# Shared cross attention: the row maxima turned by four products on column tiles instead of one transpose

## The reference

```python
q = (x @ Wq + bq)   # 16 heads of 16
k = (context @ Wk + bk)
v = (context @ Wv + bv)
scores = einsum('bhqd,bhkd->bhqk', q, k) / 4
attn = softmax(scores, axis=-1)
x = x + merge(einsum('bhqk,bhkd->bhqd', attn, v)) @ Wo + bo
```

## Time and profile before

| | |
|---|---|
| median of three executions | 1522.3 us |
| profiled execution | 1522.39 us |
| its span | 1520.6 us |
| TensorE busy | 1368.7 us, 90% |
| weight loads busy | 1059.2 us, 70% |
| DVE busy | 765.3 us, 50% |
| ACT busy | 643.5 us, 42% |
| 32 transposes of the maxima, each of three layers | 0.276 us median each |

### The profile page before, as it was taken

How to read it: one execution, slowest core, us unless ns; L and a number is a source line. 1 busy time by engine, 2 the same in 40 slices (tenths; PEclk the granted TensorE clock), 3 DMA queues, 4 the chain that set the end, 5 groups by cost and what they waited for, 6 DMA issues and landing times. The chain is left out here.

```text
span 1520.6 us, 31526 instructions
## 1 busy us (share of the span) xinstructions
PE 1368.7 (90%) x12506; PEld 1059.2 (70%) x12506; DVE 765.3 (50%) x1723; ACT 643.5 (42%) x1680; POOL 198.1 (13%) x197
## 2 busy tenths in 40 slices
PE   7999899989989899999999869989967896799887
PEld 6776667866556677879999755669964575577632
DVE  3666677655556676500000475600127485477565
ACT  3444226633366266234444235532224674166300
POOL 3000260000034300041111200040032000400000
PEclk9999999999999999899999978999998997799999
DMA  6000340011301200467994100364211000600100
GB/s 213 1 1 1 68 68 16 3 43 42 78 8 21 51 4 3 154 225 274 348 346 169 35 22 1 132 254 163 103 47 49 1 2 1 110 11 3 67 1 22
DMA packets 43943, 120.19 MB, mean 79 GB/s; under 512 B 11931, under 2 KB 28440, under 8 KB 38412
## 3 DMA queue, kind: packets, MB, share of 16 engines
q1 hardware_dynamic: 33048, 62.04, 14.2%
q0 software_dynamic: 7616, 53.12, 10.1%
q10 hardware_dynamic: 3136, 3.03, 0.6%
HBM read 95.78 MB, written 11.00 MB: 70 GB/s over the span
## 5 line engine op out<-in xcount | busy, mean ns | idle before, releaser
L798 PE MATMUL wide<-early_kt,early_q 32*100 32x361 f32 x512 | 96.6, 490 | 2.7 <-PEq L66 1.5
L2533 ACT ACTIVATE l1f_hidden<-wide,l1f_pack 128x128 f32<-128x128 f32 x160 | 58.8, 368 | 78.0 <-PE wide L2472 68.1
L2635 DVE TENSOR_TENSOR l1f_out<-summed,l1f_pack 128x256 f32<-128x256 f32 x20 | 8.5, 425 | 156.8 <-PE summed L2480 156.8
L113 PE MATMUL summed<-ident 128*128 128x128 f32 x320 | 46.8, 315 | 35.9 <-PEq L66 35.9
L2472 PEld LDWEIGHTS wide<-l1f_rt,l1f_pack 128*128 128x128 f32 x640 | 74.5, 192 | 1.8 <-issue 0.8
L2472 PE MATMUL wide<-l1f_rt,l1f_pack 128*128 128x128 f32 x640 | 74.8, 275 | 0.6 <-ACT l1f_rt L2523 0.6
L113 PEld LDWEIGHTS summed<-ident 128*128 128x128 f32 x320 | 44.8, 227 | 40.4 <-issue 40.4
L2480 PE MATMUL summed<-l1f_pack,l1f_hidden 128*128 128x256 f32 x320 | 72.4, 379 | 0.0
L1208 DVE TENSOR_REDUCE l3x_mx<-wide 100x2 f32<-100x722 f32 x64 | 55.7, 907 | 25.5 <-PE wide L798 25.5
L1208 DVE TENSOR_REDUCE l1x_mx<-wide 100x2 f32<-100x722 f32 x64 | 55.5, 907 | 20.4 <-PE wide L798 20.4
L1208 DVE TENSOR_REDUCE l0x_mx<-wide 100x2 f32<-100x722 f32 x64 | 55.4, 907 | 18.9 <-PE wide L798 18.9
(11 more groups left out here) (593 smaller groups left out, 3384.0 us busy)
## 6 DMA issues: line engine op xcount, KB each, us to landing
l2f_w<-l2f_w_dram SPq DMA_DIRECT2D x16, 1024.0 KB, 11.9
ctxt<-ctxt_dram SPq DMA_DIRECT2D x4, 1083.0 KB, 17.1
early_kt<-soon_kd SPq DMA_DIRECT2D x32, 90.8 KB, 3.3
l1f_sorted_x<-l1f_zeros SPq DMA_DIRECT2D x4, 640.0 KB
l1f_rows<-l1f_sorted_x SPq DMA_DIRECT2D x20, 128.0 KB, 7.5
l1f_sorted_y<-l1f_out ACTq DMA_DIRECT2D x20, 128.0 KB, 9.3
l0f_w<-l0f_w_dram SPq DMA_DIRECT2D x18, 128.0 KB, 2.1
l1f_shared<-l1f_shared_dram SPq DMA_DIRECT2D x1, 2180.0 KB, 8.2
```

The lines of the kernel that those rows point to most:

```text
L113: pe.matmul(net.summed[:, 1, 0:P], net.ident[:], net.ident[:], start=True, stop=True)
L798: pe.matmul(wide[0:S, i, 0:SKV], q4[R * i:R * (i + 1), g % 2, b, g // 2, :], kt[R * i:R * (i + 1), g % 2, b, g // 2, 0:SKV], start=True, s ...
L2533: act.activation(hidden[:, f, 0:P], wide[:, f % 4, 0:P], ACT.Gelu, bias=b1_of(pack[:, n % SLOTS, :], f)).then_inc(sem["h_ready"], 1)
L2635: dve.tensor_tensor(out[:, n % 2], summed[:, n % 2, 0:E], b2_of(pack[:, n % SLOTS, :]), ALU.add).then_inc(sem["y_ready"], 1)
```

## The change

The one transpose of `turn_maxima` becomes four matmuls. Head i's 32 columns of `mx` are the weights, the identity of 100 x 100 is the moving operand, and the result goes to partitions 32 i to 32 i + 31 of the same columns of the same bank: one column tile each, as in `weigh`. The numbers in the bank are the same. The semaphore comes off the last of the four.

```diff
@@ turn_maxima @@
                     pe.wait_ge(sem["m_ready"], 2 * n + 2)
                     if n >= 1:
                         pe.wait_ge(sem["p_ready"], Q * (n - 1) + 1)
-                    pe.transpose(scored[0][:, LOW:LOW + S], mx[:, n % 2, :], net.ident[0:S, 0:S]).then_inc(sem["mt_psum"], 1)
+                    for i in range(Q):
+                        last = pe.matmul(scored[0][R * i:R * (i + 1), LOW:LOW + S], mx[:, n % 2, R * i:R * (i + 1)], net.ident[0:S, 0:S], start=True, stop=True)
+                    last.then_inc(sem["mt_psum"], 1)
```

## The result

The changed kernel takes 1528.95 us, median of 20 executions (1523.98 to 1536.52), beside 1519.2 us for the kernel before, also of 20 (1506.50 to 1532.64). The ratio is 1.0068, 95% interval 1.0048 to 1.0089: slower by 10.3 us (7.3 to 13.5). The forecast was 7.9 us slower.

The account below looks back on a forecast made before the run. The loop from score through ACT's exponential and the turn to the next score was taken as the bound. 7.4 us plus 0.6 less some 0.1 gave +7.9 us, so 1530.2 us; range 1521 to 1538.

Parts of the forecast that it names:

- ACT's exponential: ACT's exponential of `turned`, which turn_maxima awaits through p_ready; forecast to release the turn, 0.11 to 0.12 us before its load.
- the turn's load: PE's first weight load of turn_maxima in each period; its start was forecast not to move.
- the drain after the sums: Tile-shape changeover between weigh's weighted sums and the turn; forecast hidden behind ACT by 0.14 us, so removing it gains nothing.
- The rival that called the drain the bound: The changeover after the weighted sums, not ACT, holds the turn: 0.20 us less per turn, 17 us faster, 1505; chance 0.07.
- two rounds: The turn's four products run as 8 records, two passes over the four column tiles, one step between them 0.085 us.
- The turn's time: From the turn's first load to the next score's load: forecast 0.24 us before, 0.315 after, +0.08 per turn.
- the spacing of the first round: Delay from first to fourth column tile in the turn's first four records, taken from the weighted sums: 0.02 us.
- The first rival: Loads issued fresh after p_ready delay the turn's second round: +0.16 us per turn, 1537; chance 0.14 with all above it.
- the row of fresh loads: Timeline row of 32-row loads issued right after a wait, 8 in 0.29 us; evidence for slower products in the turn.
- the ring: Loop of score, score_by_key, ACT's exponentials, turn and next score, 2.45 us per period; nothing else on it was to get shorter.
- Four turns of the last layer at half clock: Turns at the start of the last layer, run near half clock, priced double: 4 x 0.16 = 0.6 us.
- The sum, 7.9 us: Whole forecast slowdown: 92 turns x 0.08 = 7.4 us, 0.6 for four slow turns, some 0.1 given back.

Follow-up runs that it names:

- waits turned: Changed kernel (four products) with the score's two semaphore counts made one and p_ready's wait written before m_ready's: 1518.9 us, ratio to the kernel before 1.0017.
- the kernel with both halves swapped: Kernel before with one score count per pair and score_by_key issued ahead of the score in both halves of each period: 1695.2 us.

## Why the prediction was right

Point by point, in its own steps:

- ACT's exponential sets the turn's load, and the drain after the sums is covered by 0.13 to 0.14 us. Right. Shown by lengthening the sums (0.17 more cost 0.04), and by the kernels in which the count of ACT stands on the load itself. The rival that called the drain the bound ended here. The Trainium skill's rule in TensorEngine Tiling (Array Packing), Key Properties, that changing the tiling mode drains TensorE, would lead to it: the rule itself agrees with every trace here, the next shape's load waiting until 0.07 before the modelled end, and removing such a changeover gained nothing, since it was not the last to end.
- Four products are 8 records in two rounds. Right: 672 more records.
- The turn's time grows by 0.08 us. The mechanism was right and the term too small: it measured 0.103. The step of the sum that failed is the spacing of the first round, which I took from sums whose loads start 0.007 apart, tile by tile. After the turn's separate wait the later tiles' loads come 0.03 later: the eight start 0, 0.032, 0.036, 0.042, 0.049, 0.064, 0.071 and 0.077 after the first, and the last record at 0.161 where the sum had 0.135. With the waits turned, they start 0.007 apart as in the sums, and the same four cost 0.309 - 0.235 = 0.074. That the products are then dispatched ahead of the wait is the reading, not something a row shows. The first rival, fresh loads that delay the second round, thus had the right cause and too high a price: 0.16 over the transpose, of which 0.08 over my forecast, where 0.023 was measured. One argument against it was misread: the row of fresh loads was not near the lower clock, for the stretch from 520.70 to 521.20 has a granted clock of 1.00. Its wider loads remain.
- Nothing else on the ring moves. Right: ACT's first exponential stands 1.036 after the score's load in both kernels, and DVE's idle time stayed at 0.54 to 0.56. DVE's sum starts 0.129 after the score's load, where it was 0.117: 0.012 later and not 0.03, and it cost nothing.
- Four turns of the last layer at half clock, 0.6 us more. Not testable: where the lower clock falls differs from one execution to the next. The changed kernel's profile has one such turn in that layer, 0.66 from load to load (1340.65 to 1341.31), but there the sums ran until 1341.05, so that row is no price of the turn alone.
- The sum, 7.9 us, is 2.4 us under the measured 10.3; of these 2.1 are 93 x 0.023 of the mis-sized term. That the forecast time, 1530.2, lies 1.3 us from the measured 1528.95 is partly luck: it started from a median of three executions, 1522.3, which is 3.1 over the 1519.2 of twenty, and that hid the shortfall.

## What to carry to other kernels

Before a changeover or a wait is removed, find what else ends just before the instruction behind it; here 0.13 us of ACT's work covered it, and an experiment that lengthens the covered work tells the size of the cover. Price a replaced operation by the same shape's row in the same place behind a wait: the four products behind a wait of their own took 0.338, with the wait on the first of them 0.309. A wait that ends last belongs on the instruction itself, which here meant writing it first, and the waits that are long over ahead of it. When a median differs from what the trace's periods promise, compare the mean granted clocks before looking for a mechanism.

## What the runs showed of the hardware that was not expected

- One f32 plain product on the full array (100 rows, 128 columns, 100 moving) took 0.395 us from its load to the next shape's load, four on column tiles 0.338 and one transpose 0.235.
- The place of a wait counts: with the awaited count in a wait of its own ahead of the load, 0.113 us from the end of ACT's work to the load, with the count on the load 0.052.
- The count of a semaphore by two, in place of two counts 0.042 us apart, came 0.026 before the second of them.
- The granted clock can stay at 1.2 GHz though TensorE has a record at every moment: 130.00 us busy of 130.00, clock 0.50, in the kernel with both halves swapped, while another layer of the same run, as full of records, had 1.00. What decides between the two was not found.
